# Graph attention on one Trainium2 core: the two parts of a score added on VectorE, and only finished scores turned by TensorE

## The reference, cut to what matters

```python
h_src = h_all[edge_type, src]
h_dst = h_all[edge_type, dst]
scores = einsum('ehd,hd->eh', h_src, attn_src) + einsum('ehd,hd->eh', h_dst, attn_dst)
scores = where(scores > 0, scores, 0.2 * scores)
amax = maximum(segment_max(scores, dst), 0.0)
w = exp(scores - amax[dst])
out = segment_sum(h_src * w / denom[dst], dst)
```

## Time and profile before

| | us |
|---|---|
| median of 3 runs | 4554.82 |
| lowest and highest | 4553.86 and 4555.9 |
| the profiled execution, its own time | 4559.83 |
| its span | 4558.0 |

### The profile page before, as it was taken

One profiled execution on the slowest core, in us unless ns is written; L12 is line 12 of the kernel. 1 busy time (PEld: TensorE's weight loads), 2 busy tenths in 40 slices (PEclk: granted clock), 3 DMA queues, 4 the chain that ended last, 5 costly groups with the idle time before them and its releaser, 6 DMA issues. The chain is left out here.

```text
span 4558.0 us, 47412 instructions
## 1 busy us (share of the span) xinstructions
PE 2768.8 (61%) x12379; PEld 2184.2 (48%) x12379; DVE 2110.7 (46%) x3857; ACT 1141.0 (25%) x2893; POOL 2594.6 (57%) x2731
## 2 busy tenths in 40 slices
PE   5333433333333333434559899957887877858998
PEld 4333333333333333334447644446666666646665
DVE  7322222224222222224635344458888878864444
ACT  6101111110101111112324322234444444424222
POOL 6677777776777777774520132067777777741000
PEclk9666555665565655556679999978778888876999
DMA  4422222222221221222233355345544444430000
GB/s 130 90 53 53 54 53 53 53 53 72 53 53 53 53 53 53 53 53 96 77 118 107 111 214 194 161 143 140 139 136 140 139 135 140 139 104 22 16 16 24
DMA packets 200821, 409.75 MB, mean 90 GB/s; under 512 B 51763, under 2 KB 125123, under 8 KB 193636
## 3 DMA queue, kind: packets, MB, share of 16 engines
q0 software_dynamic: 102016, 246.46, 20.0%
q1 hardware_dynamic: 84868, 153.14, 9.7%
q10 hardware_dynamic: 13664, 6.91, 0.6%
HBM read 305.56 MB, written 104.44 MB: 90 GB/s over the span
## 5 line engine op out<-in xcount | busy, mean ns | idle before, releaser
L721 POOL DMA_INDIRECT ring<-t_gcn,idx x1564 | 1477.7, 945 | 517.6 <-issue 476.1
L782 PE MATMUL psum<-ring,big 128*128 x3328 | 751.5, 418 | 1232.6 <-SPq L729 1228.6
L782 PEld LDWEIGHTS psum<-ring,big 128*128 128x128 f32 x3328 | 699.9, 321 | 1284.2 <-issue 1284.2
L1609 POOL DMA_INDIRECT xs_ring<-t_msg,idx x832 | 797.2, 958 | 380.3 <-issue 247.1
L807 DVE TENSOR_TENSOR big<-big,psum 128x1024 f32 x208 | 254.0, 1221 | 1449.6 <-PE psum L782 1448.8
L748 ACT COPY psum<-zero_sum 128x1024 f32<-128x1024 f32 x208 | 211.0, 1015 | 1762.4 <-DVE big L807 1744.5
L1734 PE MATMUL psum<-xs_ring,a_hot 128*128 128x264 f32 x1456 | 414.6, 446 | 0.0
L1734 PEld LDWEIGHTS psum<-xs_ring,a_hot 128*128 128x128 f32 x1456 | 335.7, 231 | 76.8
L1498 PE MATMUL psum<-big,a_xnt 128*128 128x512 f32 x784 | 355.0, 596 | 0.5 <-ACT a_xnt L1470 0.5
L1403 POOL DMA_INDIRECT a_back<-t_y,m_addr x98 | 97.9, 999 | 438.6 <-POOLq L1207 279.9
L219 DVE TENSOR_TENSOR big<-dloc,psum 128x1024 f32<-128x1024 f32 x208 | 252.3, 1214 | 4.3 <-PEq L701 4.3
(11 more groups left out here) (412 smaller groups left out, 4270.5 us busy)
## 6 DMA issues: line engine op xcount, KB each, us to landing
t_msg<-a_rows SPq DMA_DIRECT2D x49, 1056.0 KB, 3.9
a_near<-t_near SPq DMA_DIRECT2D x52, 512.0 KB, 4.1
ring<-t_gcn,idx POOLq DMA_INDIRECT x1564, 2.5
m_xin<-t_tok SPq DMA_DIRECT2D x105, 128.0 KB, 2.1
t_y<-m_yb SPq DMA_DIRECT2D x105, 128.0 KB, 2.1
xs_ring<-t_msg,idx POOLq DMA_INDIRECT x832
xs_ring<-in_x SPq DMA_DIRECT2D x7, 896.0 KB, 11.5
t_xs<-xs_ring SPq DMA_DIRECT2D x7, 896.0 KB, 6.4
```

The lines of the kernel that those rows point to most:

```text
L721: g.indirect_dma_start(out=ring[:, p % HALF_RING * 8 + j, :], out_offset=None, in_=t_gcn[conv], in_offset=bass.IndirectOffsetOnAxis(ap=idx ...
L782: m = t.matmul(opened[:, bass.ds(to[j], ROW_BYTES)].bitcast(F32), hot[q % 2][:, j, :], ring_bytes[:, bass.ds(at[j], ROW_BYTES)].bitcast(F3 ...
L1609: g.indirect_dma_start(out=ring[:, slot, :, :].rearrange("p h c -> p (h c)"), out_offset=None, in_=t_msg, in_offset=bass.IndirectOffsetOnA ...
```

## The change

The sum moves from PE to VectorE and the leaky step moves ahead of the turn. `score(n)` now waits for the rows and for `pick`, adds the gathered part onto `edst` in place, makes the leaky step from SBUF into a new tile `score_of`, and signals. PE transposes `score_of` (one instruction in the place of two accumulating matmuls), ScalarE copies the turned scores from PSUM straight into `scoret`, and `within_steps` waits for that copy. `plain` is gone. The order of functions on each engine is as it was.

```diff
@@ scalar
-                                a.wait_ge(s_cross.sem, cross(k, "sum"))
-                                if k:
-                                    a.wait_ge(s_chain.sem, chain(k - 1, "score"))
-                                a.copy(plain[:], ps[1][:, 0:P]).then_inc(s_plain.sem, 1)
+                                a.wait_ge(s_cross.sem, cross(k, "sum"))
+                                a.copy(scoret[:], ps[1][:, 0:P]).then_inc(s_turned.sem, 1)
@@ tensor
-                                for h in range(2):
-                                    half = 2 * (k % RB) + h
-                                    t.wait_ge(s_row[half].sem, s_row[half].base + 128 * (k // RB + 1))
-                                t.wait_ge(s_picked.sem, s_picked.base + 2 * k + 2)
                                 if k:
                                     t.wait_ge(s_cols.sem, s_cols.base + k)
-                                t.matmul(ps[1][:, 0:P], ring[:, slots(k), :, HD].rearrange("p j h -> p (j h)"), ident[:], start=True, stop=False)
-                                t.matmul(ps[1][:, 0:P], edst[k % 2][:].rearrange("p j h -> p (j h)"), ident[:],
-                                         start=False, stop=True).then_inc(s_cross.sem, 1)
+                                t.wait_ge(s_chain.sem, chain(k, "score"))
+                                t.transpose(ps[1][:, 0:P], score_of[:].rearrange("p j h -> p (j h)"), ident[:]).then_inc(s_cross.sem, 1)
@@ vector, pick
                             if n >= 2:
-                                v.wait_ge(s_cross.sem, cross(n - 2, "sum"))
+                                v.wait_ge(s_chain.sem, chain(n - 2, "score"))
@@ vector
                         def score(n):
-                            v.wait_ge(s_plain.sem, s_plain.base + n + 1)
+                            for h in range(2):
+                                half = 2 * (n % RB) + h
+                                v.wait_ge(s_row[half].sem, s_row[half].base + 128 * (n // RB + 1))
+                            v.wait_ge(s_picked.sem, s_picked.base + 2 * n + 2)
+                            v.tensor_tensor(edst[n % 2][:], edst[n % 2][:], ring[:, slots(n), :, HD], ALU.add).then_inc(s_chain.sem, 1)
                             if n:
-                                v.wait_ge(s_cross.sem, cross(n - 1, "diff"))
-                            v.scalar_tensor_tensor(scoret[:], ps[1][:, 0:P], 0.2, plain[:], ALU.mult, ALU.max).then_inc(s_chain.sem, 1)
+                                v.wait_ge(s_cross.sem, cross(n - 1, "sum"))
+                            v.wait_ge(s_chain.sem, chain(n, "whole"))
+                            v.scalar_tensor_tensor(score_of[:], edst[n % 2][:], 0.2, edst[n % 2][:], ALU.mult, ALU.max).then_inc(s_chain.sem, 1)
 
                         def within_steps(n):
                             v.wait_ge(s_links[n % 3].sem, s_links[n % 3].base + n // 3 * 16 + 16)
-                            v.wait_ge(s_chain.sem, chain(n, "score"))
+                            v.wait_ge(s_turned.sem, s_turned.base + n + 1)
```

More of the change, by code:

```diff
@@ L1540, in gnn_ffn_kernel @@
                 edst = [sb(f"a_edst{k}", [P, SBS, HEADS], F32, ph) for k in range(2)]
-                plain = sb("a_plain", [P, P], F32, ph)
+                score_of = sb("a_score_of", [P, SBS, HEADS], F32, ph)
                 scoret = sb("a_scoret", [P, P], F32, ph)
@@ L1560, in gnn_ffn_kernel @@
                     sig(f"s_{k}") for k in ("linked", "chain", "whole", "rescaled", "cross"))
-                s_plain, s_runs, s_carry, s_fade, s_cols, s_soft, s_scaled, s_back = (
-                    sig(f"s_{k}") for k in ("plain", "runs", "carry", "fade", "cols", "soft", "scaled", "back"))
+                s_turned, s_runs, s_carry, s_fade, s_cols, s_soft, s_scaled, s_back = (
+                    sig(f"s_{k}") for k in ("turned", "runs", "carry", "fade", "cols", "soft", "scaled", "back"))
                 s_zero = sig("s_zero")
@@ L1565, in gnn_ffn_kernel @@
                 s_links = [sig(f"s_links{k}") for k in range(3)]
-                CHAIN = ("score", "fwd", "bwd", "ahead", "behind", "left", "right", "top", "fall", "less")
+                CHAIN = ("whole", "score", "fwd", "bwd", "ahead", "behind", "left", "right", "top", "fall", "less")
                 CROSS = ("sum", "rows", "cols", "diff")
```

## The result

The changed kernel takes 4588.69 us (median of 4 runs, 4585.01 to 4589.7), the kernel before 4555.27 us (4 runs, 4553.86 to 4555.9). The ratio is 1.0071, with a 95% interval of 1.0059 to 1.0083: 33 us slower. The profiled execution took 4585.01 us, with a span of 4583.2; it is the shortest of the four. Its attention began 4.0 us earlier than in the trace of before (the first gather at 2978.22 instead of 2982.25); the change touches nothing ahead of that.

A forecast was written before the change was run, and what follows sets the result against it. POOL's gathers, 20.14 us a block, were taken as the bound; VectorE's loop of 19.78 grew to 20.22, then 20.46, taken as 20.45. Lag 14 us, minus 3.1, plus 0.1 gave 4566 us; own range 4558 to 4576, outer 4554 to 4590.

The forecast's parts named there:

- The lag: Attention blocks, from block 6 on: each 0.31 us over POOL's 20.14, adding up to 14 us at block 51.
- The loop's own length: Attention block, score to score: 20.45 us taken, against POOL's 20.14.
- W to scan: From VectorE finishing weigh(2p), called W, to its first scan: 0.40 us becomes 1.50 when VectorE is late.
- take nothing: VectorE's new add, strided read of the gathered column: bounds nothing to 0.1 us more, costed at nothing.
- W to message: From W to PE's first message when VectorE is late: about 0.25 us becomes 1.25.
- at nothing by itself: PE: two accumulating matmuls gone for one transpose, about 1.1 us where PE waits anyway, costed at nothing.
- the clock that the sum added 0.24 for: PE's first message: one block in eight falls to the lower clock, taking the block from 20.22 to 20.46 us.
- rival 1: Attention: gathers stay the bound, VectorE's loop stays at 19.78 to 20.14, time 4555 to 4560 us; chance 0.31.
- The range's upper end: Attention block length: at most 21.52 us, block 16's path with the new start of the message.
- Rival 2: PE's messages stay at the lower clock, 7.2 us each: 4589 us for half the blocks, 4619 for all; chance 0.15.
- the 3.1 that come back at the reload: Stage's end: the lag moves the first reload past the last gather, ending their collision and returning 3.1 us.
- Its price: POOL's gathers meeting VectorE's two-SBUF-input operations: 0.11 us a meeting, 0 to 0.1 per block, 0 to 5 us.

The follow-up runs named there:

- the cures: Changed kernel with registers loaded ahead of PE's wait for the scores (1.0074), with 12 filler matmuls ahead of the turn (1.0018, 1.0012), or with both (1.0001).
- the kernel before with filler: Kernel before with 12 identity matmuls, result unread, on PE between the turn of the finished scores and the next block's sum: 1.0039.
- the kernel with VectorE's path longer: Kernel before with four more VectorE operations between the score and the first scan, into a tile nobody reads: 1.0001.

## Why the prediction was right, and where it was off

**How close it came.** The forecast was 4566 us, with a range of its own of 4558 to 4576 and an outer range of 4554 to 4590. 4588.69 lies in the outer range alone, 1.3 us below its end, and the loss is three times the one forecast (33 us, not 11). The direction and the mechanism in the large were right; the size was not.

**The bound.** That POOL paces the loop at 20.14 us, that the other engines are close to it, and that the change moves the pace to their own loop held: VectorE waits for no rows from block 2 on, and POOL waits for PE. (PE's slices of the stage read 7 to 8 tenths on the profile's page, not 8 to 9 as said ahead of the prediction; nothing rests on it.) The lag begins with block 1, not with block 6.

**The loop's own length.** 20.45 was forecast, and 20.49 is what 28 blocks show. That hit is luck in good part. W to scan was to be 1.50 and is 1.69 (3899.69 to 3901.38): the add takes 0.38, not 0.29, so to "take nothing" for the strided column was wrong and its upper bound of 0.1 right; the step between the two operations is 0.10, not 0.05; the turn takes 0.45, the upper end. For a late VectorE W to scan had been 0.31, not the 0.40 that was read from an early block. W to message was to be 1.25 and is 1.93: of the 0.68 too little, 0.55 are the register load and branch, for which the sum had 0.10. To cost the two accumulating matmuls that are gone from PE "at nothing by itself" is the step that failed: under them PE's sequencer prepared the message. Against this, the clock that the sum added 0.24 for did not get worse on average: L1732 takes 439 ns, L1734 took 446 in the profile of before, and the granted clock is 0.81 to 0.83 in each ten blocks from block 1 on.

These errors do not simply cancel, since the sum goes along VectorE's path, and the block hangs on the message's end. Put the forecast's own 1.25 in place of 1.93 on that path and a regular block is an estimated 20.49 - 0.68 = 19.8 us, below POOL's 20.14. POOL would then pace most blocks still, and the outcome would have been nearer to rival 1. By this estimate the 0.68 us are the greater part of the loss.

**The irregular blocks.** The sum had them as one block in eight at the lower clock, spread evenly. They come as four places and the start, and cost 15.1 us in all. The kernel before has messages of 5.8 us too, in blocks 14 to 17, and there the message begins 0.25 us after W, a block takes 20.2 to 20.5 us, and VectorE has it back by block 21. In the changed kernel the message begins 1.93 us after W or later, such a block takes 22.0 to 22.4, and nothing is won back. The range's upper end, 1.25 + 20.27 = 21.52, was the right path for them with the wrong start: with 1.93 it is 22.20. The 15.1 are most of the 22 us that lie between 4566 and 4588.69. Rival 2 (4589 for half the blocks) had the size and not the mechanism: not half of the blocks but four of fifty ran the whole first message at the lower clock, and their neighbours a part of it, on top of my own forecast.

**Lag and end.** 14 us of lag were forecast and 33.1 measured; the 3.1 that come back at the reload are there (3.3). POOL waits for PE, as said, but not in the last ten blocks above all: the waits of over 0.6 us lie between 3385 and 3785 us, the longest (2.2 to 2.4) right behind irregular blocks.

**The other rivals.** Rival 1 (the gathers stay the bound) is refuted by the 0.0 ahead of L1812. Its price, the contention of VectorE's two-input operations with POOL, is small: a gather takes 960 ns instead of 954. The rule that the prediction took from the Trainium skill, TensorE: Matmul & The Clock Gate, Part 4, that a transpose does not count as activity the way a matmul does, is not borne out: 24 transposes raised the granted clock to 0.85 just as 24 matmul instructions did. The measurement decides.

**What is shown and what argued.** Shown by the two traces of the first comparison: in both kernels a block's length is the time from W to the end of the first message and 12.8 to 13.2 us more, so the later message accounts for the longer blocks. Shown by the experiments: a late first message alone costs what the change costs; taking the turn off VectorE brings nearly nothing; the register load costs 0.8 us of the message's start in each block; keeping PE at work removes nearly all of the cost. Argued: that in the first comparison too the 0.65 us ahead of the message are the register load, for which its trace has the same gap, and that the cures would help there as much. Open are what stops the engines where the kernel before takes 5205 us and more, what the floor of 24 us there is, and why the low clock comes in just those four places.

## What to carry to other kernels

A wait that is moved to another engine must be costed on both sides: the result's new way round (VectorE, PE, ScalarE, VectorE), and what stands behind the moved wait in each queue, register loads and branches included, since the work that was removed may have been what they hid under. An average slack is not a slack: where an engine was on average 0.1 us late and only hidden by others' work, taking that work away turns every late block into lag. In this kernel what PE does first after an idle gap of 4 us ran at the lower clock, and should have been costed so. A loop of several engines has to be judged by its longest way round, not by busy shares: look for the pair of events whose distance is the same in every block. And a group's mean can mix two kinds: the first and the second message had to be read apart to see what the filler did.

## What the runs showed that was not expected

- PE's load of eight registers and the branch on one of them stand for 0.6 to 0.8 us between two instructions, and for nothing if the load stands ahead of a wait that takes longer anyway.
- Transposes keep the granted clock as high as matmuls do (0.85 for both).
- Filler ahead of one piece of work can leave the lower clock to another: in the kernel before with filler the first message took 3.28 us and the second 5.0, where the kernel with VectorE's path longer had 5.2 and 3.28.
- VectorE's add of a column with a stride of 33 numbers takes 381 ns where the dense subtraction of the same size takes 292.
- The same kernel took 4555 us in the first comparison and 5205 to 5218 on the three chips of the experiments, with waits of up to 7.7 us for a releaser that the profile calls remote, and the same change cost 0.7% in the one and 1.9% in the other.
